# A state space layer's feed-forward, closing norm, next norm and router made one phase of chunks passed from engine to engine

## The reference

```python
x1 = layernorm(x + mamba2(x)) * n1_g + n1_b
t  = x1 + gelu(x1 @ ffn_w1 + ffn_b1) @ ffn_w2 + ffn_b2      # FF = 512
h  = h + (layernorm(t) * n3_g + n3_b)                        # closing norm, residual
xn = layernorm(h)                                            # next norm
logits = xn @ Wr + br                                        # router of 8 experts
```

## Time and profile before

| | us |
|---|---|
| median of 3 runs (1600.42 to 1610.35) | 1603.69 |
| the profiled execution's own time | 1606.4 |
| its span, first to last instruction | 1604.6 |
| PE busy in the span | 1335.1 |
| DVE busy | 807.8 |
| ACT busy | 737.7 |
| POOL busy | 352.2 |

### The profile page before, as it was taken

The page is one execution under the profiler, slowest core; times in us unless marked ns, Lnnn a source line. Parts: engine busy times, 40 slices in busy tenths (PEclk is TensorE's granted clock), DMA queues, the critical chain, the costliest instruction groups (busy, mean ns, idle before and its releaser), DMA issues. The chain is left out here.

```text
span 1604.6 us, 35141 instructions
## 1 busy us (share of the span) xinstructions
PE 1335.1 (83%) x11047; PEld 1161.7 (72%) x11047; DVE 807.8 (50%) x2632; ACT 737.7 (46%) x2600; POOL 352.2 (22%) x696
## 2 busy tenths in 40 slices
PE   6999579999964999462576999958997997589996
PEld 3777479999954999462575888848996886378884
DVE  0488531111144777437652555555332777557774
ACT  0588344444412555321242666624441786135553
POOL 0256411000010566413471000011000110110010
PEclk9999689999977999785697999979998899599998
DMA  6000010000001000002321000000000000100001
GB/s 225 13 1 0 1 34 27 13 26 13 0 1 40 2 0 0 14 1 64 116 48 51 1 0 0 1 9 25 20 7 32 2 0 1 38 1 1 0 0 31
DMA packets 27274, 34.49 MB, mean 21 GB/s; under 512 B 5673, under 2 KB 20212, under 8 KB 26932
## 3 DMA queue, kind: packets, MB, share of 16 engines
q1 hardware_dynamic: 22804, 26.13, 5.1%
q10 hardware_dynamic: 2784, 4.47, 0.8%
q0 software_dynamic: 1600, 2.82, 0.7%
HBM read 29.84 MB, written 4.03 MB: 21 GB/s over the span
## 5 line engine op out<-in xcount | busy, mean ns | idle before, releaser
L464 ACT ACTIVATE a_E<-quad_bank,a_shift 108x108 f32<-108x108 f32 x704 | 236.8, 356 | 3.9 <-DVE a_shift L528 3.4
L979 ACT ACTIVATE f_hid<-quad_bank,f_b1s 128x512 f32<-128x512 f32 (+1 forms) x240 | 148.0, 645 | 187.2 <-PE quad_bank L910 187.0
L1024 DVE SCALAR_TENSOR_TENSOR f_y<-bank,GATE,f_y 128x128 f32<-128x128 f32 x288 | 81.0, 344 | 253.0 <-PE bank L923 252.8
L923 PEld LDWEIGHTS bank<-f_w2s,f_hid 128*128 128x128 f32 x1728 | 201.7, 192 | 3.7
L923 PE MATMUL bank<-f_w2s,f_hid 128*128 128x128 f32 x1728 | 203.2, 275 | 0.0
L910 PE MATMUL quad_bank<-f_xp,f_w1p 128*128 128x512 f32 (+1 forms) x720 | 167.7, 382 | 16.6 <-DVE f_xp L1005 16.6
L910 PEld LDWEIGHTS quad_bank<-f_xp,f_w1p 128*128 128x128 f32 x720 | 125.1, 192 | 37.4 <-issue 8.5
L464 ACT ACTIVATION_READ_ACCUMULATOR a_E<-quad_bank,a_shift 108x1 f32 x704 | 150.3, 214 | 0.0
L358 PE MATMUL bank<-a_xT,a_wqk 128*128 128x108 f32 x1056 | 141.2, 286 | 1.4 <-ACT a_xT L482 1.4
L301 POOL TENSOR_TENSOR a_ve<-a_mv,const 108x1 f32<-108x1 f32 x88 | 16.7, 190 | 558.8 <-DVE a_mv L597 558.8
L358 PEld LDWEIGHTS bank<-a_xT,a_wqk 128*128 128x128 f32 x1056 | 131.9, 200 | 6.9 <-issue 4.3
(11 more groups left out here) (317 smaller groups left out, 2415.2 us busy)
## 6 DMA issues: line engine op xcount, KB each, us to landing
pats<-in_patches SPq DMA_DIRECT2D x3, 1296.0 KB, 18.5
pats<-in_patches ACTq DMA_DIRECT2D x2, 1296.0 KB, 15.0
f_w1s<-in_f_w SPq DMA_DIRECT2D x8, 256.0 KB, 2.7
f_w2s<-in_f_w SPq DMA_DIRECT2D x8, 256.0 KB, 3.2
f_w1a<-in_f_w SPq DMA_DIRECT2D x1, 2048.0 KB, 10.4
f_w2a<-in_f_w SPq DMA_DIRECT2D x1, 2048.0 KB, 14.8
out<-H SPq DMA_DIRECT2D x1, 1134.0 KB
a_f_in<-in_a_factors SPq DMA_DIRECT2D x1, 1088.0 KB, 5.6
```

Source lines behind the costliest of these rows:

```text
L464: e = act.activation(E[:, q, n, :], scores[:, n // tiles, n % tiles, :], ACT.Exp, scale=w.scale, bias=shift[:, q, n:n + 1], accum_out=tota ...
L923: mm = pe.matmul(m.bank[n % 2][0:W, g * D:(g + 1) * D], hid[:, n % 2, c, g * W:(g + 1) * W], w2s[:, u, c * 128:(c + 1) * 128], start=(c == ...
L979: act.activation(hid[:, n % 2, c, 0:k * W], m.quad_bank[:, (n * chunks + c) % 4, 0:k * W], func, bias=b1s[:, u, c:c + 1]).then_inc(hid_rea ...
L1024: ins = dve.scalar_tensor_tensor(out=h, in0=y[:, (g - c0) * D:(g - c0 + 1) * D], scalar=m.GATE[:, bass.ds(e + g * 8, 1)], in1=h, op0=ALU.m ...
```

## The change

The three phases after the state space part become one, `ffn_phase`. It is a pipeline over chunks: in step s PE does `up` of chunk s, the transposes of chunk s-4, `down` of s-1 and the router products of s-4; DVE adds and takes statistics of `T` for s-2, and adds to `H` and takes its statistics for s-3; POOL makes a scale and a shift from each of the statistics (four small operations instead of two) and multiplies by n3_g; ACT does both normalizations (`Identity` with scale and shift, one operation a group) besides the gelu and the copies. PE starts with ten products that keep it busy.

The split of the feed-forward's input moves into the state space phase: ACT writes its copy as the high part `XP[:, 0]`, and DVE makes the rest `XP[:, 1]` from `t_bank` in a new last piece of its step, `live(t, 7)`. `t_bank` is then in use until DVE has read it, so PE's transpose waits for `t_split` in place of `t_ready`. The depth of the pipeline is 8 in place of 7.

```diff
--- before.py
+++ after.py
-        depth = 7
+        depth = 8
...
                 if live(t, 6):
                     g = t - 6
                     pe.wait_ge(scaled, g * 3 + 2)
-                    at_least(pe, t_ready, g)
+                    at_least(pe, t_split, g)
                     pe.transpose(t_bank[:, 0:P], tt[:, par, :], m.ident[0:P, 0:P]).then_inc(t_psum, 1)
...
                 if live(t, 6):
                     g = t - 6
                     act.wait_ge(t_psum, g + 1)
-                    act.activation(m.XT[:, bass.ts(g, P)], t_bank[:, 0:P], ACT.Copy).then_inc(t_ready, 1)
+                    act.activation(m.XP[:, 0, bass.ts(g, P)], t_bank[:, 0:P], ACT.Copy).then_inc(t_ready, 1)
...
                     dve.bn_aggr(mv[:, par, :], bn6[:, par, :]).then_inc(stats, 1)
+                if live(t, 7):
+                    g = t - 7
+                    dve.wait_ge(t_ready, g + 1)
+                    dve.tensor_tensor(m.XP[:, 1, bass.ts(g, P)], t_bank[:, 0:P], m.XP[:, 0, bass.ts(g, P)], ALU.subtract).then_inc(t_split, 1)
             steps(dve, step, depth)
...
-def close_phase(nc, m):
...
+def ffn_phase(nc, m, io, rows):
...
+        def _(sp):
+            sp.dma_start(w1s[:, :], io["fs_w1"].rearrange("e p n -> (e p) n")).then_inc(w1_loaded, 16)
+            sp.dma_start(b1s[:, :], io["fs_b1"].rearrange("e p n -> (e p) n")).then_inc(loaded, 16)
+            sp.dma_start(w2s[:, :], io["fs_w2"].rearrange("e p n -> (e p) n")).then_inc(loaded, 16)
+            sp.dma_start(wr[:, :], io["f1_router"]).then_inc(loaded, 16)
+            for n, (c, k) in enumerate(CHUNKS):
+                sp.wait_ge(xn_ready, n + 1)
+                sp.dma_start(rows[c * P:(c + k) * P, :].rearrange("(g p) d -> p g d", p=P),
+                             m.XN[:, c * D:(c + k) * D].rearrange("p (g d) -> p g d", d=D)).then_inc(rows_stored, 16)
...
         @block.gpsimd
         def _(pool):
-            inverse_deviations(pool, m, mv, rstd, stats_ready, var_eps, rstd_ready)
-            for n, (c, k) in enumerate(CHUNKS):
-                pool.wait_ge(normed, n + 1)
-                x = m.T[:, c * D:(c + k) * D].rearrange("p (g d) -> p g d", d=D)
-                pool.tensor_tensor(x, x, wide("n3_g", k), ALU.mult).then_inc(scaled, 1)
+            pool.wait_ge(w1_loaded, 16)
+            pool.tensor_tensor(w1p[:, 0, :], w1s[:, :], m.one.broadcast_to([128, hid_n]), ALU.mult).then_inc(w_high, 1)
+            pool.wait_ge(w_high, 1)
+            pool.tensor_tensor(w1p[:, 1, :], w1s[:, :], w1p[:, 0, :], ALU.subtract).then_inc(w_split, 1)
...
+            def scale_shift(n, mv, scale, shift, stats, own, ready):
...
+                s, b = scale[:, c:c + k], shift[:, c:c + k]
+                pool.wait_ge(stats, n + 1)
+                pool.tensor_tensor(s, col(1), m.eps[0:P, :].broadcast_to([P, k]), ALU.add).then_inc(own, 1)
+                pool.wait_ge(own, n * 3 + 1)
+                pool.tensor_tensor(s, s, m.mhalf[0:P, :].broadcast_to([P, k]), ALU.pow).then_inc(own, 1)
+                pool.tensor_tensor(b, col(0), m.minus[0:P, :].broadcast_to([P, k]), ALU.mult).then_inc(own, 1)
+                pool.wait_ge(own, n * 3 + 3)
+                pool.tensor_tensor(b, b, s, ALU.mult).then_inc(ready, 1)
+            for s in range(nb + 4):
+                if 0 <= s - 2 < nb:
+                    scale_shift(s - 2, t_mv, t_scale, t_shift, t_stats, t_steps, t_rstd)
+                if 0 <= s - 3 < nb:
+                    scale_shift(s - 3, h_mv, h_scale, h_shift, h_stats, h_steps, h_rstd)
+                if 0 <= s - 2 < nb:
+                    c, k = CHUNKS[s - 2]
+                    pool.wait_ge(t_normed, s - 1)
+                    x = m.T[:, c * D:(c + k) * D].rearrange("p (g d) -> p g d", d=D)
+                    pool.tensor_tensor(x, x, wide("n3_g", k), ALU.mult).then_inc(t_scaled, 1)
...
+            def up(n):
+                c0, k = CHUNKS[n]
+                for c in range(4):
+                    i = n * 4 + c
+                    if i >= 4:
+                        pe.wait_ge(hid_ready, i - 3)
+                    for a, b in PARTS:
+                        mm = pe.matmul(m.quad_bank[:, i % 4, 0:k * P], w1p[:, a, c * 128:(c + 1) * 128],
+                                       m.XP[:, b, c0 * P:(c0 + k) * P], start=((a, b) == PARTS[0]), stop=((a, b) == PARTS[-1]))
+                    mm.then_inc(hid_psum, 1)
+            def down(n):
+                c0, k = CHUNKS[n]
+                pe.wait_ge(hid_ready, (n + 1) * 4)
+                if n > 1:
+                    pe.wait_ge(t_sum, n - 1)
+                for g in range(k):
+                    for c in range(4):
+                        mm = pe.matmul(m.bank[n % 2][0:P, g * D:(g + 1) * D], hid[:, n % 2, c, g * P:(g + 1) * P],
+                                       w2s[:, c * 128:(c + 1) * 128], start=(c == 0), stop=(c == 3))
+                mm.then_inc(y_psum, 1)
+            def turn(n):
+                c, k = CHUNKS[n]
+                pe.wait_ge(xn_ready, n + 1)
+                at_least(pe, xt_ready, n)
+                for g in range(k):
+                    mm = pe.transpose(m.bank[3][:, g * P:(g + 1) * P], m.XN[:, (c + g) * D:(c + g + 1) * D], m.ident[0:P, 0:P])
+                mm.then_inc(xt_psum, 1)
...
+            def route(n):
+                c, k = CHUNKS[n]
+                pe.wait_ge(xt_ready, n + 1)
+                for g in range(c, c + k):
+                    mm = pe.matmul(m.bank[2][0:P, g * 8:(g + 1) * 8], m.XT[:, g * P:(g + 1) * P], wr[:, :], start=True, stop=True)
+                mm.then_inc(lg_psum, 1)
+            keep_busy(pe, m, m.quad_bank[:, 0, :], 10)
+            pe.wait_ge(w_split, 1)
+            pe.wait_ge(loaded, 48)
+            for s in range(nb + 4):
+                if s < nb:
+                    up(s)
+                if 0 <= s - 4 < nb:
+                    turn(s - 4)
+                if 0 <= s - 1 < nb:
+                    down(s - 1)
+                if 0 <= s - 4 < nb:
+                    route(s - 4)
...
+            act.wait_ge(loaded, 48)
+            def gelu(n):
+                c0, k = CHUNKS[n]
+                for c in range(4):
+                    act.wait_ge(hid_psum, n * 4 + c + 1)
+                    if n > 1 and c == 0:
+                        act.wait_ge(y_psum, n - 1)
+                    act.activation(hid[:, n % 2, c, 0:k * P], m.quad_bank[:, (n * 4 + c) % 4, 0:k * P], ACT.Gelu,
+                                   bias=b1s[:, c:c + 1]).then_inc(hid_ready, 1)
...
+            def norm(n, dst, src, scale, shift, ready, normed):
+                c, k = CHUNKS[n]
+                act.wait_ge(ready, n + 1)
+                for g in range(c, c + k):
+                    a = act.activation(dst[:, g * D:(g + 1) * D], src[:, g * D:(g + 1) * D], ACT.Identity,
+                                       scale=scale[:, g:g + 1], bias=shift[:, g:g + 1])
+                a.then_inc(normed, 1)
+            for s in range(nb + 4):
+                if 0 <= s - 4 < nb:
+                    norm(s - 4, m.XN, m.H, h_scale, h_shift, h_rstd, xn_ready)
+                if s < nb:
+                    gelu(s)
+                if 0 <= s - 4 < nb:
+                    c, k = CHUNKS[s - 4]
+                    act.wait_ge(xt_psum, s - 3)
+                    act.activation(m.XT[:, c * P:(c + k) * P], m.bank[3][:, 0:k * P], ACT.Copy).then_inc(xt_ready, 1)
+                if 0 <= s - 2 < nb:
+                    norm(s - 2, m.T, m.T, t_scale, t_shift, t_rstd, t_normed)
...
         @block.vector
         def _(dve):
-            group_statistics(dve, m.T, bn6, mv, stats_ready)
             for c, k in CHUNKS:
                 h = m.H[:, c * D:(c + k) * D].rearrange("p (g d) -> p g d", d=D)
                 ins = dve.tensor_tensor(h, h, wide("n3_b", k), ALU.add)
             ins.then_inc(moved, 1)
-            dve.wait_ge(stats_ready, len(CHUNKS))
-            for n, (c, k) in enumerate(CHUNKS):
-                dve.wait_ge(rstd_ready, n + 1)
+            dve.wait_ge(moved, 1)
+            def statistics(n, src, bn6, mv, done):
+                c, k = CHUNKS[n]
                 for g in range(c, c + k):
-                    x = m.T[:, g * D:(g + 1) * D]
-                    ins = dve.tensor_scalar(x, x, mv[:, g, 0:1], rstd[:, g:g + 1], ALU.subtract, ALU.mult)
-                ins.then_inc(normed, 1)
-            dve.wait_ge(moved, 1)
-            for n, (c, k) in enumerate(CHUNKS):
-                dve.wait_ge(scaled, n + 1)
-                h = m.H[:, c * D:(c + k) * D]
-                dve.tensor_tensor(h, h, m.T[:, c * D:(c + k) * D], ALU.add).then_inc(h_done, 1)
-            dve.wait_ge(h_done, len(CHUNKS))
+                    dve.bn_stats(bn6[:, g, :], src[:, g * D:(g + 1) * D])
+                dve.drain()
+                for g in range(c, c + k):
+                    ins = dve.bn_aggr(mv[:, g, :], bn6[:, g, :])
+                ins.then_inc(done, 1)
...
+            for s in range(nb + 4):
+                if 0 <= s - 2 < nb:
```

(40 more changed lines are left out.)

31 lines of the change are left out of this document (22 added, 9 removed).

## The result

The changed kernel takes 1628.55 us (median of 4 runs, 1620.66 to 1631.59) where the kernel before, on the same chip, takes 1604.22 (1600.42 to 1610.35): a ratio of 1.0122, with a 95% interval of 1.0085 to 1.0159.

What follows compares the result with a forecast made beforehand. PE was taken to bound the state space loop, no single engine the stretch from feed-forward to router. 1604.6 + 30.2 (loop waits, drain, end) - 29.7 (merged phase) = 1605.1, put on the runs' median as 1604; range 1592 to 1619.

Steps and rivals of the forecast that it cites:

- second rival: State space loop: gaps of 1.8 us in 8.4 drop PE's clock to 0.50, adding 93 us, so 1697; chance 0.07.
- the sum: Whole span: 1604.6 + 30.2 lost in the state space phase - 29.7 gained after it = 1605.1, a change of +0.5.
- The ring: State space loop: PE's transpose waits for DVE's last-placed split, DVE for PE's projection; 1.79 us lost a step.
- the wait: PE's transpose held for DVE's split in steps 7 to 21: 15 x 1.79 = 26.9 us lost.
- the branch: Hardware loop's branch: PE's queue can no longer run ahead; 6 rounds by 0 to 0.45, taken as 1.4 us.
- Drain and end: Steps 22 to 27 lose 1.5 us (0 to 10.7); after the last copy, one split and hand-over lose 0.4.
- The new phase: Feed-forward to router as one pipeline: logits 50.6 us after PE's start, 30.9 earlier than before; gain 29.7 (25 to 33).
- company: Merged phase: DVE's sums of H slowed beside POOL's work, 0.2 for each of six, 1.2 us (0 to 4.7).
- That the loop doesn't slow: First rival, state space loop: PE's rows hide room for the added wait, only the gain is left, 1574; chance 0.08.
- That the phase passes chunks badly: Third rival, merged phase: queues wait for wrong chunks or engines block; gain 18 in place of 29.7, 1616; chance 0.15.

## Why the prediction was wrong, step by step

**The rival that was set aside: the clock.** This is the step that failed. The prediction named it (second rival, 0.07, "PE's clock falls in the loop"), and dismissed it by rows 5: "in the sorted experts PE was busy 7.40 of 10 us with gaps up to 1.80 us, and the clock stayed 1.00". Those rows are two different places: the gap of 1.80 ends at 820.12, the window is 830 to 840, where the largest gap is 1.12. The window before 820, in which the large gap lies, is at 1.00 too, so the reading as such holds. But the inference went from one gap of that length to one in every step. Nor does PE's busy share tell the two stages apart: the window of rows 5 has 7.40 of 10 us at 1.00, and a step of the loop, at full clock but between two slow ones, has more (6.88 of 8.52 from 596.74 on). The runs show what did make a difference: the same 1.80 with the same neighbours goes at 1.00 or not, by whether one product of 0.43 us more stands in each step. The price was also mis-sized. The rival had only the case of the whole stage at 0.50, +93, and so looked unlikely; what came is a fall of 3 to 4 us in seven of the steps, at 1.6 to 1.7 each, and a longer one that costs 3.3, 13 to 15 us in all where the sum had nothing. A partial case was missing between nothing and everything. The Trainium skill, TensorE: Matmul & The Clock Gate, "A second HAM failure mode: psum-queue depth-cycling", tells of a kernel whose PE idles briefly but frequently between groups of products, so that the clock goes back and forth between its two levels. This trace agrees (0.54 from 588 to 590, 1.00 from 590 to 596), and the prediction should have set that section against rows 5.

**The ring.** Right in mechanism, place and nearly in size: forecast 26.9 for the wait and 1.4 for the branch, 28.3; measured with the clock held, 30.9. The cycle from the start of the projection to the start of the transpose was put at 2.23; it is 2.24 and 2.40 in the loop (583.69 to 585.93, 594.34 to 596.74), where it had been 0.44, so 1.80 and 1.96 are lost. The idle times in the rows (1.64 and 1.80) are shorter, as they count from the projection's modelled end. Ahead of the loop the idle time is only 1.29, so three steps cost 1.52 each and not 1.79. In the loop a step costs 2.19 more than before on average. The term of the branch is what was too small: behind it PE idles 0.30 to 0.38 for issue, and no longer overlaps the transpose with the next product, so that this product starts 0.59 to 0.66 behind the transpose and not 0.10; in a pair of steps (17.67 in place of 13.24) that makes 4.4, where 2 x 1.79 and the branch made 3.8. The split took 0.27, the lower bound, where 0.32 was chosen.

**Drain and end.** 1.6 and 0.3 measured, 1.5 and 0.4 forecast. Right, though the 1.5 was chosen between 0 and 10.7, so that its closeness is in part luck.

**The new phase.** Right. The logits come 50.9 after PE's start (50.6), and the whole is 31.4 shorter, where the sum had 30.9 less 1.2 for company. It was right with one price that was off: ACT's norm of four groups takes 1.65 instead of 1.14. Rows 10 are activations from PSUM with a bias alone, and these read SBUF with a scale and a shift; which of the differences makes it longer no run separates. Only its last two groups (0.88) stand on the path. Of company between DVE and POOL nothing is to be seen on POOL's products (1.27 here, 1.30 in rows 8), but the first small operation beside a sum of `H` took 0.55 in place of 0.20, four times in the phase, and ended each time with the sum. So here POOL waits for DVE, which agrees with what the prediction cites of the Trainium skill, SBUF — State Buffer, "Who interferes with whom"; the size is 0.35 in each of the four places, 1.4 in all, where the prediction had put 0.7 and 2.8.

**The rivals otherwise.** That the loop doesn't slow is refuted by the steps of 8.1 to 9.2 at full clock. That the phase passes chunks badly is refuted too. The sum without the clock is +30.9 + 1.6 + 0.3 - 31.4 = +1.4, and the kernels with a busy product measured +0.2% (3 us). The clock adds 15, and 1604 + 1.4 + 14.9 is 1620, just past the range; the other 1.6 and 4.1 of the first comparison lie outside the stretch that was changed.

What stays open: the 4.1 us behind the logits in the first comparison. The layers there are unchanged. From the logits to the end of the span the kernel before takes 849.1 and the kernel after 853.2, but the same kernel takes 861.3 in the repeat, and all the traces together 843.6 to 861.3; so 4.1 us are within what this stretch varies by. What it varies with is not known. Nor do the runs say why a gap in every step and one gap elsewhere differ for the clock, or how much work a step needs for it to hold: without the product it falls, with one it holds, and nothing lies between.

## What to carry to other kernels

Before an instruction is made the last in an engine's step, ask which engine waits for it and what it stands behind. A short operation (0.27 us) behind this step's statistics closed a ring through two queues and cost 30.9 us; the same operation ten places earlier in the queue cost nothing. Where an engine is full, a new wait on it can cost twice: its own length, and on TensorE also the clock, for which a single gap elsewhere in the trace is no evidence; price a partial fall, too. And look at what else the next stage waits for: the split moved out of the feed-forward had run beside the load and split of the weights, which end 1.3 us earlier, so moving it could win 1.3 us at most.

## What was not expected of the hardware

TensorE's granted clock fell to its lower level behind waits of 1.64 to 1.80 us that came back in every step of 8.5 to 9.2 us, in 8 of 11 steps, and returned within the step (0.54 from 588 to 590, 1.00 from 590 to 596). Behind the first such wait, of 1.81 at 577.41, it had not yet fallen. One product of 0.43 us in each step, at either side of the wait, kept it at 1.00, and made the 15 steps 13 to 15 us faster (in front of the wait) or 9 to 11 us (behind it), though PE did more. In steps ahead of the loop, with waits of 1.29, it stayed at 1.00. A hardware loop's branch, cheap as long as an engine's queue runs ahead, cost PE 0.30 to 0.38 us of issue time in every round once the last instruction ahead of it waited.
